# Four graph layers on one core: layer 2 mixes nodes before the product with W, takes its logits from dot products on VectorE, and every engine's blocks stand in another order

## The chip, the core and the metric
The kernel runs on one core of a Trainium2 chip. The metric is the device time of one execution in microseconds (us). Engine names in the profile: PE is TensorE (PEld its weight loads), DVE is VectorE, ACT is ScalarE, POOL is GpSimd, SP is SyncE.

## The reference
The input x is 128 graphs of 128 nodes with 256 features, adj is 128 dense 128 x 128 matrices. Four residual layers follow each other, each on `h = max(layernorm(x), 0)`. The change touches the second:

```python
Wh = jnp.einsum('bsi,io->bso', hidden_state, W)
Wh1 = Wh @ a[:OUT_F, :]
Wh2 = Wh @ a[OUT_F:, :]
e = Wh1 + jnp.swapaxes(Wh2, 1, 2)
e = jax.nn.leaky_relu(e, negative_slope=ALPHA)
attention = jnp.where(adjacent_matrix > 0.5, e, NEG_INF)
attention = jax.nn.softmax(attention, axis=1)
h_prime = jnp.einsum('bst,bto->bso', attention, Wh)
return jax.nn.elu(h_prime)
```

The first layer is a hypergraph convolution with a 512-wide hidden layer (W1, W2), the third a diffusion with three weight matrices, the fourth weights a value product by a softmax over the nodes. All of it is fp32.

## The kernel before
Graphs are taken in 32 groups of four. In round i the kernel works on five groups at once: `next` (group i+1: degrees of the hypergraph, normalised x, the product yT), `front` (group i: layer 1 and layer 2), `mid` (i-1: layer 3), `late` (i-2: first part of layer 4) and `tail` (i-3: its softmax, sum and store). Each engine has one `body(r)` in which the blocks of these groups stand in an order written out by hand, and it runs them strictly in that order; semaphores counted in graphs hold a block until its inputs exist and its buffer or PSUM bank (`BANK`) is free. `rounds` runs `first`, then rounds 0 to 3 unrolled, a loop, and the last four unrolled.

Products with weights go as three passes of fp32r (`split_product`: high with high, high with low, low with high), so every transposed activation is kept as a high part, which ScalarE copies out of PSUM, and a low part, which VectorE subtracts (`low_of_relu`, L1239). Products of two activations and transposes are plain fp32 (L328, L491, L400).

Layer 2 of `front` runs like this. VectorE adds the residual (L1478), takes the moments (L1329, L1333) and writes the centred h (L1347) in `front_ln1`. TensorE transposes h (`front_h1`, eight 128 x 128 transposes, L491), ScalarE and VectorE make h1T high and low (L885, L1239), TensorE multiplies by W with the two columns W a appended (`front_wh`, 24 matmuls of 258 columns), VectorE scales the two logit columns (`front_columns`, L1513), ScalarE scales wh (`keep_wh`, L851). TensorE spreads one logit column over the partitions (`front_b1`, L400), VectorE forms logits, leaky relu and maximum (L1496, L1502, L1508), ScalarE the exponential (L940), VectorE scales the weights (`front_scale`, L1524), and TensorE applies them to wh (`front_att`, four fp32 products of 256 columns). The elu (L1412, L945, L1419) and layer 3's norm follow, and TensorE transposes layer 3's h (`mid_h2`) behind the four blocks `front_w1`. GpSimd does the rsqrts (`rsqrt`: L1083, L1085) and the elementwise sums, two tensors from SBUF each (L1090 to L1141). In VectorE's and SyncE's order `adj_f` of the next group is loaded only when `front_penalty` (L1378) has read the old one.

## Time and profile before
| what | value |
|---|---|
| time, median of 3 runs (lowest, highest) | 1487.95 us (1487.61, 1488.96) |
| profiled execution, first to last instruction | 1487.0 us |
| busy TensorE, VectorE, ScalarE, GpSimd | 96%, 81%, 66%, 64% |
| chain that ended last: TensorE, ScalarE, VectorE | 75%, 11%, 5% |
| granted TensorE clock | 0.989 of full |

The profile's page and its views show one execution, whose span of 1487.0 us is 0.95 us under the median of the runs. Busy shares are averages; an instruction's length includes a fixed part that overlaps its neighbour, so what an instruction costs its engine is the distance from start to start in the timeline.

### The profile page before, as it was taken

Reading aid. Unit: us, or ns where it says so; the run is one execution under the profiler, and the core shown is the slowest. Engines: PE = TensorE matmul, PEld = TensorE weight load, DVE = VectorE, ACT = ScalarE, POOL = GpSimd, SP = SyncE. Lnnn points to the kernel's source line nnn. Section 1 sums busy time; section 2 is a strip of 40 time slices with the busy share of each in tenths; the row PEclk is TensorE's granted clock in tenths of the full one; section 3 lists DMA queues with packets and bytes.
Section 4 is the critical chain, followed back from the end, with each engine's and each line's share of the span. In section 5 each row is a group of like instructions: output and inputs, shape, how many; then the busy total and the mean of one; then the engine's idle time right before and its main releaser. Section 6 shows DMA issues by size and latency. Waiting matters only on the chain.

```text
span 1487.0 us, 33717 instructions
## 1 busy us (share of the span) xinstructions
PE 1423.5 (96%) x8920; PEld 1263.7 (85%) x8920; DVE 1206.8 (81%) x4621; ACT 978.8 (66%) x2122; POOL 949.7 (64%) x974
## 2 busy tenths in 40 slices
PE   6799999999999999999999999999999999999975
PEld 5679988889888988988888988888988888988864
DVE  5778888888888888888888888888888888888773
ACT  4456667766667776667776666776666776666754
POOL 4555775666776666676666676675677666677524
PEclk9899999999999999999999999999999999999997
DMA  4001111101111110111110111110111110111001
GB/s 128 22 15 37 37 42 44 49 32 46 35 48 36 49 47 30 35 49 35 49 49 28 42 42 35 49 49 28 45 39 35 49 49 28 49 35 41 23 29 50
DMA packets 75372, 62.01 MB, mean 42 GB/s; under 512 B 3014, under 2 KB 70986, under 8 KB 75339
## 3 DMA queue, kind: packets, MB, share of 16 engines
q1 hardware_dynamic: 75338, 61.63, 12.7%
q8 instruction: 14, 0.23, 0.1%
q14 instruction: 20, 0.16, 0.0%
HBM read 36.45 MB, written 16.78 MB: 36 GB/s over the span
## 4 chain that ended last, share of the span: by engine, by line
PE 75%; ACT 11%; issue 5%; DVE 5%; DMA 1%; POOL 0%; DVEq 0%; ACTq 0%; POOLq 0%; SPq 0%
PE ps L343 35%; PE ps L347 18%; PE ps L328 16%; PE ps L491 4%; ACT wh L851 3%; ACT pT L940 3%; ACT h L918 2%; ACT h2T_hi L881 1%; ACT p L929 1%; PE ps L400 1%; ACT yT_hi L953 1%; DMA x_in<-in_x 1%; DVE stats L1329 1%; DVE h L1347 1%; DVE binc_T L1368 0%
## 5 line engine op out<-in xcount | busy, mean ns | idle before, releaser
L1130 POOL TENSOR_TENSOR x3n<-p,x 128x512 f32<-128x512 f32 x64 | 80.8, 1285 | 252.8 <-ACT p L929 252.8
L851 ACT ACTIVATE p<-ps,rs 128x512 f32<-128x512 f32 (+1 forms) x256 | 138.2, 582 | 106.4 <-PE ps L347 73.7
L1090 POOL TENSOR_TENSOR hT_lo<-hT,hT_hi 128x512 fp32r<-128x512 f32 x126 | 162.8, 1294 | 68.5 <-ACT hT_hi L871 65.4
L1085 POOL TENSOR_TENSOR rs<-var_e,neg_half 128x4 f32<-128x4 f32 x160 | 164.9, 1031 | 23.7
L343 PE MATMUL ps<-wl_hi,h2T_hi 128*128 128x258 f32 (+1 forms) x512 | 148.5, 371 | 7.8 <-ACT h2T_hi L881 7.2
L328 PE MATMUL ps<-p,alT 128*128 128x256 f32 (+1 forms) x512 | 136.9, 390 | 3.3 <-DVE h3T_lo L1239 2.3
L343 PE MATMUL ps<-wl_lo,h2T_hi 128*128 128x258 f32 (+1 forms) x512 | 132.9, 341 | 0.0
L347 PE MATMUL ps<-wl_hi,h2T_lo 128*128 128x258 f32 (+1 forms) x512 | 132.4, 340 | 0.0
L949 ACT ACTIVATE h3T_hi<-ps 128x512 fp32r<-128x512 f32 x64 | 38.0, 594 | 139.0 <-PE ps L491 138.9
L491 PE MATMUL ps<-ident,h 128*128 128x128 f32 x768 | 118.3, 278 | 9.9 <-DVE h L1347 9.4
L491 PEld LDWEIGHTS ps<-ident,h 128*128 128x128 f32 x768 | 92.3, 142 | 32.9 <-issue 10.4
L1347 DVE TENSOR_SCALAR_CACHE_REDUCE h<-x,mv 128x256 f32<-128x256 f32 x256 | 113.6, 463 | 2.3
L1329 DVE BATCH_NORM_STATS2 stats<-x 128x6 f32<-128x256 f32 x256 | 109.2, 426 | 5.5
L1117 POOL TENSOR_TENSOR alT<-zb,adj_m 128x512 f32<-128x512 f32 x32 | 41.1, 1285 | 113.1 <-DVE zb L1438 113.1
L328 PEld LDWEIGHTS ps<-p,alT 128*128 128x128 f32 x512 | 86.4, 190 | 15.7 <-issue 4.8
L343 PEld LDWEIGHTS ps<-wl_hi,h2T_hi 128*128 128x128 f32 x512 | 81.0, 191 | 21.2 <-issue 17.0
L347 PEld LDWEIGHTS ps<-wl_hi,h2T_lo 128*128 128x128 f32 x512 | 88.5, 190 | 11.6
L343 PEld LDWEIGHTS ps<-wl_lo,h2T_hi 128*128 128x128 f32 x512 | 88.4, 190 | 11.3
L851 ACT ACTIVATE vqk<-ps,rs 128x384 f32<-128x384 f32 x128 | 73.9, 577 | 33.8 <-PE ps L347 33.7
L871 ACT ACTIVATE hT<-ps,cols_sb 128x512 f32<-128x512 f32 x128 | 88.1, 689 | 6.6 <-PE ps L347 1.5
L1105 POOL TENSOR_TENSOR x<-x 128x512 f32<-128x512 f32 x64 | 82.0, 1282 | 13.3 <-ACT x L851 13.3
L871 ACT ACTIVATE hT_hi<-ps,cols_sb 128x512 fp32r<-128x512 f32 x128 | 87.6, 684 | 0.1
(178 smaller groups left out, 4476.0 us busy)
## 6 DMA issues: line engine op xcount, KB each, us to landing
x_in<-in_x SPq DMA_DIRECT2D x32, 512.0 KB, 3.9
out_x<-x SPq DMA_DIRECT2D x32, 512.0 KB, 2.9
adj_f<-in_adjT SPq DMA_DIRECT2D x32, 256.0 KB, 2.9
adj_m<-in_adjT SPq DMA_DIRECT2D x32, 256.0 KB, 2.8
adj_l<-adj_m SPq DMA_DIRECT2D x32, 256.0 KB, 2.3
vqk<-in_l_wk SPq DMA_DIRECT2D x3, 256.0 KB, 5.2
x<-in_w2T SPq DMA_DIRECT2D x1, 512.0 KB, 5.1
x<-in_w1T SPq DMA_DIRECT2D x1, 512.0 KB, 5.9
```

Source lines behind the costliest of these rows:

```text
L328: last = pe.matmul(dst, lhsT(c), rhs(c), start=(c == 0), stop=(c == chunks - 1))
L343: pe.matmul(dst, lhsT(a, c), rhs(b, c), start=(a == b == c == 0), stop=False)
L347: last = pe.matmul(dst, lhsT(1 - late, c), rhs(late, c), start=False, stop=(c == chunks - 1))
L491: last = pe.transpose(bank(name, b)[:, ((g % 2) * KC + c) * P:((g % 2) * KC + c + 1) * P], h[:, g, c * P:(c + 1) * P], ident[:])
L851: return act.activation(dst, src, ACT.Copy, scale=scale)
L871: act.activation(dst[:, hc, :], bank("u", hc), ACT.Relu, bias=cols_sb[:, 0, hc:hc + 1]).then_inc(S[ready], 1)
L1085: pool.tensor_tensor(rs[:, layer, :], var_e[:, layer, :], neg_half[:], ALU.pow).then_inc(done, G)
L1090: pool.tensor_tensor(hTs[1][:, hc, :], hT[:, hc, :], hTs[0][:, hc, :], ALU.subtract).then_inc(S["hT_lo"], 1)
L1105: pool.tensor_tensor(x4[:, s], x4[:, s], x3[:, s], ALU.add).then_inc(S["x4_ready"], 2)
L1130: pool.tensor_tensor(x3n[:, s], p0[:, s], x2[:, s], ALU.add).then_inc(S["x3_ready"], 2)
L1329: dve.bn_stats(stats[:, layer, g, :], src[:, g, :]).then_inc(st, 1)
L1347: dve.tensor_scalar(dst[:, g, :], src[:, g, :], mv[:, layer, g, 0:1], None, ALU.subtract, ALU.add, accum_out=unread[:, layer, g:g + 1]).th ...
```

## The change
Layer 2 is regrouped: softmax(e) (h W) is computed as (softmax(e) h) W. ScalarE now writes h1r = relu(x1 - mean) (`centre`), TensorE multiplies it by the attention weights straight into transposed form (`front_mix`, eight fp32 products of 128 columns), and `front_att` becomes the three-pass product with W (24 matmuls of 256 columns). `front_h1`, `front_wh` and `keep_wh` are gone. The two logits of a node are dot products of h1r with rows of W a that were spread over all partitions once (`va`, made by `third_rows`): `front_dots`, eight instructions on VectorE per round with both operands in SBUF. The rsqrt of the norm goes into the logits and into the softmax weights (one more small multiplication per pair). Moments of layers 1, 3 and 4 are taken in pairs of graphs. PSUM banks are dealt out anew, many waits are dropped, round 0 has a list of its own (`opening`), VectorE's body begins with `next_count` and ends with work of the next round (`ahead`), and GpSimd's begins with work of the round before (`past`).

```diff
-        BANK = {"u": (0, 4, 3, 2), "y": (0, 7), "s": (4, 5), "d": (0,), "c2": (6, 5), "h1": (7, 1), "wh": (2, 3, 4,
-                5), "b1": (6,), "att": (1, 5), "h2": (4, 3), "p2": (4, 5, 6, 7), "p10": (7, 6, 7, 6), "b2": (5,),
-                "z": (1, 2, 3, 4), "ap": (0, 1, 2, 3), "az": (0, 3), "h3": (0, 5), "vqk": (4, 1, 6, 7), "ak": (6,),
-                "row": (1,), "turn": (7,)}
+        BANK = {"u": (6, 7, 0, 3), "y": (7, 6), "s": (5, 6), "d": (7,), "c2": (1, 3), "b1": (5,), "att": (3, 1),
+                "h2": (1, 7), "p2": (4, 5, 6, 7), "p10": (2, 7, 4, 3), "b2": (0,), "z": (1, 2, 3, 4),
+                "ap": (0, 1, 2, 3), "az": (0, 4), "h3": (5, 6), "vqk": (5, 6, 4, 5), "ak": (5,),
+                "row": (0,), "turn": (2,), "yA": (1, 2)}
...
+            def load_x(r):
+                if not r.steady and r.i in (0, 1,):
+                    wait(sp, S["h0_ready"], r.front(G))
+                if not r.steady and r.i in (0, 1,):
+                    wait(sp, S["xb_ready"], r.front(G))
+                sp.dma_start(x_in[:], group(x, r.i + 1)).then_inc(S["x_loaded"], 16)
...
+            def third_rows(r):
+                pe.wait_ge(S["dotted"], 2 * KC)
+                for k in range(2):
+                    for c in range(KC):
+                        last = spread(ps[:, 5, (k * KC + c) * P:(k * KC + c + 1) * P], att_cols[:, c, k:k + 1])
+                last.then_inc(S["va_spread"], 1)
...
-            def front_h1(r, b):
-
...
-            def front_wh(r, g):
...
-                split_product(bank("wh", g)[:, 0:D + 2], lambda a, c: h1Ts[a][:, g, c, :],
-                              lambda b, c: wl1s[b][:, c, :], KC,
-                              0, (S["h1T_lo"], r.front(2 * (g // 2) + 2))).then_inc(S["wh_ready"], 1)
+            def front_mix(r, b):
+                for g in (2 * b, 2 * b + 1):
+                    pe.wait_ge(S["h1_ready"], r.front(g + 1))
+                    pe.wait_ge(S["pT_scaled"], r.front(g + 1))
+                    for c in range(KC):
+                        at = ((g % 2) * KC + c) * P
+                        last = product(bank("yA", b)[:, at:at + P], lambda k: h1r[:, g, c * P:(c + 1) * P],
+                                       lambda k: pT[:, g, :], 1)
+                    last.then_inc(S["h1T_ready"], 1)
 
             def front_b1(r):
-
+                wait(pe, S["vqk_copied"], r.late(1))
                 pe.wait_ge(S["wh12_ready"], r.front(G))
...
             def front_att(r, g):
-
-                pe.wait_ge(S["wh_kept"], r.front(g + 1))
-                pe.wait_ge(S["pT_scaled"], r.front(g + 1))
-                if g == 0:
-                    wait(pe, S["h1T_lo"], r.front(G))
-                elif g == 2:
-                    wait(pe, S["wh_kept"], r.front(G))
-                product(bank_pair("att", g), lambda c: pT[:, g, :],
-                        lambda c: wh[:, g, :], 1).then_inc(S["att_ready"], 1)
+                if not r.steady and r.i == 0:
+                    pe.wait_ge(S["weights_lo"], 1)
+                pe.wait_ge(S["h1T_copied"], r.front(2 * (g // 2) + 2))
+                split_product(bank_pair("att", g), lambda a, c: h1Ts[a][:, g, c, :], lambda b, c: wl1s[b][:, c, :], KC,
+                              0, (S["h1T_lo"], r.front(2 * (g // 2) + 2))).then_inc(S["att_ready"], 1)
...
-            def keep_wh(r, g):
-
-                wait(act, S["att_ready"], r.mid(g + 1))
-                act.wait_ge(S["wh12_ready"], r.front(G))
-                scaled(wh[:, g, :], bank("wh", g)[:, 0:D], rs[:, 1, g:g + 1]).then_inc(S["wh_kept"], 1)
+            def relu_p0(r, b):
+                s = slice(2 * b, 2 * b + 2)
+                act.wait_ge(S["vb_ready"], r.mid(2 * b + 2))
+                act.activation(p0[:, s], p0[:, s], ACT.Relu).then_inc(S["relu_ready"], 2)
...
+            def centre(layer, src, dst, b, value, ready, done):
+                act.wait_ge(ready, value(2 * b + 2))
+                for g in (2 * b, 2 * b + 1):
+                    act.activation(dst[:, g, :], src[:, g, :], ACT.Relu,
+                                   bias=nmean[:, layer, g:g + 1]).then_inc(done, 1)
+
+            def front_centre(r, b):
+                centre(1, x1, h1r, b, r.front, S["nm1_ready"], S["h1_ready"])
...
+            def moments(layer, src, gs, value, st, ag):
...
+                dve.wait_ge(st, value(gs[-1] + 1))
                 dve.memset(c0[:, 0:1], 0.0).then_inc(S["filled"], 1)
...
+            def spread_about(layer, src, b, value, st, ag, done):
+                gs = slice(2 * b, 2 * b + 2)
+                moments(layer, src, (2 * b, 2 * b + 1), value, st, ag)
+                dve.wait_ge(ag, value(2 * b + 2))
+                dve.tensor_scalar(nmean[:, layer, gs], mv[:, layer, gs, 0], -1.0, None, ALU.mult).then_inc(done, 2)
...
-            def front_penalty(r):
-
-                dve.wait_ge(S["adj_f_loaded"], r.loads(r.i))
+                moments(0, x_in, range(G), r.next, S["st0"], S["ag0"])
+
+            def next_penalty(r):
+                dve.wait_ge(S["adj_f_loaded"], r.loads(r.i + 1))
...
+            def front_residual(r, b):
+                s = slice(2 * b, 2 * b + 2)
+                dve.wait_ge(S["res0_ready"], r.front(2 * b + 2))
+                dve.wait_ge(S["c2_ready"], r.front(2 * b + 2))
+                dve.tensor_tensor(x1[:, s, :], bank("c2", b).rearrange("p (g d) -> p g d", g=2),
+                                  res0[:, s, :], ALU.add).then_inc(S["x1_ready"], 2)
+
+            def front_ln1(r, b):
+                dve.wait_ge(S["x1_ready"], r.front(2 * b + 2))
+                spread_about(1, x1, b, r.front, S["st1"], S["ag1"], S["nm1_ready"])
...
+            def front_dots(r, b):
+                flat = q[:].rearrange("p g c -> p (g c)")
+                for g in (2 * b, 2 * b + 1):
+                    dve.wait_ge(S["h1_ready"], r.front(g + 1))
+                    for k, done in enumerate((S["dot_a"], S["dots_ready"])):
+                        if g > 0:
+                            dve.wait_ge(done, r.front(g))
+                        dve.tensor_tensor_reduce(flat[:, k * D:(k + 1) * D], h1r[:, g, :], va[:, k * D:(k + 1) * D],
+                                                 1.0, 0.0, ALU.mult, ALU.add,
+                                                 wh12r[:, g, k:k + 1]).then_inc(done, 1)
+
             def front_columns(r):
                 dve.wait_ge(S["rs1_ready"], r.front(G))
-                dve.wait_ge(S["wh_ready"], r.front(G))
-                dve.tensor_tensor(wh12[:], four("wh")[:, :, D:D + 2], rs[:, 1, :].rearrange("p (g a) -> p g a", a=1)
+                dve.wait_ge(S["dot_a"], r.front(G))
+                dve.wait_ge(S["dots_ready"], r.front(G))
+                dve.tensor_tensor(wh12[:], wh12r[:], rs[:, 1, :].rearrange("p (g a) -> p g a", a=1)
                                   .broadcast_to((P, G, 2)), ALU.mult).then_inc(S["wh12_ready"], G)
 
             def front_inverse(r, b):
                 s = slice(2 * b, 2 * b + 2)
                 dve.wait_ge(S["pT_ready"], r.front(2 * b + 2))
-                dve.reciprocal(rz[:, s], zsum[:, s]).then_inc(S["rz_ready"], 2)
+                dve.reciprocal(rz[:, s], zsum[:, s]).then_inc(S["rz_a"], 2)
+                dve.wait_ge(S["rz_a"], r.front(2 * b + 2))
+                dve.tensor_tensor(rz[:, s], rz[:, s], rs[:, 1, s], ALU.mult).then_inc(S["rz_ready"], 2)
```

The new order of TensorE: w1 (0 to 2), h2 (0), w1 (3), h2 (1), p2 (0, 1), row, p10 (0), w2 (0), p2 (2, 3), w2 (1, 2), w2_low (0), b2, w2 (3), w2_low (1 to 3), sums, h3 (0, 1), p10 (1), s (0, 1), c2 (0 to 3), turn, p10 (2, 3), ap (0), vqk (0), d, ap (1 to 3), vqk (1), b1, y (0), vqk (2, 3), y (1), az (0 to 2), mix (0), az (3), mix (1), ak, att (0 to 3).

The new order of VectorE: next_count, tail_max, next_inverse, late_ln3 (1), mid_columns, next_binc, next_moments, tail_norm, mid_edges, front_variance, late_low (0, 1), front_z (0 to 3), next_degrees, front_residual (0, 1), front_ln1 (0, 1), tail_out, front_dots (0, 1), front_columns, next_gt, z1_scale, front_logits (0, 1), front_leaky (0), mid_z1 (0), front_max (0), front_leaky (1), mid_z1 (1), front_max (1), mid_z1 (2), front_weights (0), mid_z1 (3), front_weights (1), y_low (0), front_low (0), mid_vb (0, 1), front_low (1), y_low (1), elu_low (0), mid_vb (2, 3), elu_high (0), elu_low (1), mid_ln2 (0), elu_high (1), mid_ln2 (1), mid_low (0), next_penalty, tail_weights, tail_sum, late_ln3 (0), mid_low (1).

The new order of GpSimd: add_res0 (0), then of the round before add_xb (1), add_x4 (1), add_bias (1), add_x3 (0), then add_res0 (1), add_x3 (1), mid_scale, front_lo (0 to 3), add_squares (0, 1), join_squares, next_scale, front_scale0, mask_edges, shift_x, late_scale, add_bias (0), front_scale1, add_xb (0), add_x4 (0).

## Rows read from the trace of the kernel before

**Rows 1.** The page, busy time of TensorE and VectorE over the span.
```profile
PE 1423.5 (96%) x8920; PEld 1263.7 (85%) x8920; DVE 1206.8 (81%) x4621; ACT 978.8 (66%) x2122; POOL 949.7 (64%) x974
```

**Rows 2.** The view by windows: rounds 3 to 30, then the rest (columns: window, length, busy time and count of each engine, clock, DMA).
```profile
146.32:1387.08 1240.76, 1226.60 (x7786) 1095.76 (x7785) 1040.04 (x4005) 849.99 (x1848) 824.60 (x841) 1.00 0.13 42
...
1387.08:1487.00 99.92, 74.97 (x414) 63.24 (x412) 58.54 (x206) 51.96 (x111) 44.26 (x43) 0.89 0.10 32
```

**Rows 3.** TensorE's timeline, one steady round: start, length, instruction (four lines, the h1 transposes around one product of h3).
```profile
709.66 0.60 PE L491 MATMUL ps<-ident,h 128*128 128x128 f32 x4
...
710.02 0.60 PE L343 MATMUL ps<-wl_hi,h3T_hi 128*128 128x384 f32 x2
...
710.46 0.51 PE L343 MATMUL ps<-wl_lo,h3T_hi 128*128 128x384 f32 x2
...
711.15 0.60 PE L491 MATMUL ps<-ident,h 128*128 128x128 f32 x4
```

**Rows 4.** TensorE's timeline, same and next round: y products, attention product, h2 and h3 transposes.
```profile
716.59 1.05 PE L328 MATMUL ps<-gt,h 128*128 128x128 f32 x8
...
717.48 1.03 PE L328 MATMUL ps<-p,alT 128*128 128x256 f32 x4
...
720.13 1.04 PE L328 MATMUL ps<-wh,pT 128*128 128x256 f32 x4
...
721.32 1.10 PE L328 MATMUL ps<-wh,pT 128*128 128x256 f32 x4 [0.15 <-ACT wh L851]
...
727.84 1.20 PE L491 MATMUL ps<-ident,h 128*128 128x128 f32 x8
...
729.28 0.70 PE L343 MATMUL ps<-wl_hi,h2T_hi 128*128 128x512 f32 x2 [0.24 <-ACT h2T_hi L881]
...
744.21 0.60 PE L491 MATMUL ps<-ident,h 128*128 128x128 f32 x4
...
745.04 1.11 PE L328 MATMUL ps<-p,alT 128*128 128x257 f32 x4 [0.23 <-DVE h3T_lo L1239]
```

**Rows 5.** VectorE's timeline, same round: last aggregate of layer 1, first elu, the longest of five waits.
```profile
708.64 0.17 DVE L1333 BATCH_NORM_AGGREGATE mv<-stats 128x2 f32<-128x6 f32 x1
...
721.48 0.68 DVE L1412 SCALAR_TENSOR_TENSOR el<-ps,x 128x512 f32<-128x512 f32 x1
...
733.69 0.29 DVE L1356 TENSOR_SCALAR_CACHE_REDUCE inc_T<-adj_f 128x128 f32<-128x128 f32 x1 [1.68 <-DMA adj_f<-in_adjT]
```

**Rows 6.** VectorE's timeline, opening: two of the dot products with one operand in PSUM, and a wait.
```profile
24.79 0.41 DVE L1276 CUSTOM_DVE_ANT_0 zb<-p,ps 128x256 f32<-128x256 f32 x1
...
25.24 0.42 DVE L1276 CUSTOM_DVE_ANT_0 zb<-p,ps 128x256 f32<-128x256 f32 x1
...
32.59 0.29 DVE L1356 TENSOR_SCALAR_CACHE_REDUCE inc_T<-adj_f 128x128 f32<-128x128 f32 x1 [5.07 <-DMA adj_f<-in_adjT]
```

**Rows 7.** VectorE by line and form, all rounds: leaky relu of q, and centring.
```profile
L1502 DVE SCALAR_TENSOR_TENSOR pT<-q 128x256 f32<-128x256 f32 x64 | 26.6, 416 | 0.1
...
L1347 DVE TENSOR_SCALAR_CACHE_REDUCE h<-x,mv 128x256 f32<-128x256 f32 x256 | 113.6, 463 | 2.3
```

**Rows 8.** VectorE's timeline, opening: instructions with both operands, or one at double rate, in SBUF.
```profile
22.16 1.01 DVE L1235 TENSOR_TENSOR hT_lo<-hT,hT_hi 128x512 fp32r<-128x512 f32 x1 [1.94 <-ACT hT_hi L871]
...
23.63 1.24 DVE L1235 TENSOR_TENSOR hT_lo<-hT,hT_hi 128x512 fp32r<-128x512 f32 x1 [0.46 <-ACT hT L871]
...
26.69 0.83 DVE L1378 TENSOR_SCALAR pen<-adj_f 128x512 f32<-128x512 f32 x1
```

**Rows 9.** GpSimd's timeline, opening: beside them.
```profile
22.57 1.75 POOL L1136 TENSOR_TENSOR res<-xb,h 128x512 f32<-128x512 f32 x1
```

**Rows 10.** GpSimd's timeline, one steady round: from layer 1's rsqrt on.
```profile
709.38 1.04 POOL L1085 TENSOR_TENSOR rs<-var_e,neg_half 128x4 f32<-128x4 f32 x1
...
710.39 1.30 POOL L1141 TENSOR_TENSOR p<-p,bk 128x512 f32<-128x512 f32 x1
...
711.63 1.30 POOL L1122 TENSOR_TENSOR xb<-x_in,b2m 128x512 f32<-128x512 f32 x1
```

More of the change, by code:

```diff
@@ new lines, in store, with hand_adj, load_mask @@
+            def store(r):
+                sp.wait_ge(S["x4_ready"], r.tail(G))
+                sp.dma_start(group(out, r.i - 3), x4[:]).then_inc(S["stored"], 16)
+            def hand_adj(r):
+                wait(sp, S["al_ready"], r.mid(G))
+                wait(sp, S["ak_ready"], r.late(G))
+                sp.dma_start(adj_l[:], adj_m[:]).then_inc(S["adj_l_loaded"], 16)
+            def load_mask(r):
+                if r.steady or r.i > 0:
+                    sp.wait_ge(S["adj_l_loaded"], r.loads(r.i - 1))
+                sp.dma_start(adj_m[:], group(adjT, r.i)).then_inc(S["adj_m_loaded"], 16)
@@ L841, in first @@
                 next_y(r, 1)
-                first_rows(r)
             pe.wait_ge(S["consts_made"], 4)
-            rounds(pe, body, first)
+            rounds(pe, body, opening, first)
         @block.scalar
@@ L1073, in first @@
                 l1_hi()
-            rounds(act, body, first)
+            rounds(act, body, opening, first)
         @block.gpsimd
@@ L1175, in body @@
             def body(r):
+                past = r.later(-1)
+                if r.has_front:
+                    add_res0(r, 0)
+                if past.has_next:
+                    add_xb(past, 1)
+                if past.has_tail:
+                    add_x4(past, 1)
+                if past.has_mid:
+                    add_bias(past, 1)
+                    add_x3(past, 0)
+                if r.has_front:
+                    add_res0(r, 1)
+                if past.has_mid:
+                    add_x3(past, 1)
+                if r.has_mid:
+                    mid_scale(r)
                 if r.has_front:
@@ L1227, in _ @@
             constants()
-            rounds(pool, body, first)
+            rounds(pool, body, opening, first)
         @block.vector
```

895 lines of the change are left out of this document (428 added, 467 removed).

## Prediction, made before the changed kernel ran

> **What bounds the kernel now.** I read the page's busy shares first, then the windows by round, then TensorE's and VectorE's timelines of one steady round, and last GpSimd's. TensorE is busy 96% of the span [rows 1]. Rounds 3 to 30 take 1240.76 us, 44.31 each, at the full clock (1.00); per round TensorE is busy 43.8 us, VectorE 37.1, ScalarE 30.4, GpSimd 29.5 [rows 2]. A busy TensorE is not one at its peak, so I take its blocks from start to start. Four transposes and six matmuls of 384 columns fill 1.49 us; four of the matmuls take 0.69, six 1.04, so four transposes cost 0.45 [rows 3]. Priced so, one round holds 42.3 us of TensorE work and 2.0 of stalls. Three stalls stand out: eight transposes of h2 last until the next product starts 1.44 us later instead of 0.90 (0.5 lost, ScalarE's copy of h2T); two attention products take 1.19 where 0.86 is the price of the like-sized product before them (0.3, keep_wh); the last h3 transposes take 0.83 instead of 0.45 (0.4, VectorE's h3T_lo) [rows 4]. TensorE sets the round; VectorE has 7.2 us free.
>
> **The change, part by part.**
>
> TensorE. `front_h1` goes: -0.90 us. `front_att` as four fp32 products (1.72) becomes `front_mix`, eight of 128 columns, priced by the y products of the same form, 0.89 for four [rows 4]: +0.06. The 24 passes with W lose two columns each, nothing. The three stalls go: behind h2 (1) now stand p2 (0, 1), which need only the pair copied before w1 (3); keep_wh is gone; between h3 and ap stand p10 (1) and s. Together TensorE would need 41.5 us of work and some 0.4 of small losses, 41.9.
>
> VectorE. From the first elu (721.48) to the last aggregate of layer 1 in the next round (708.64 + 44.51) lie 31.7 us [rows 5], of which 3.5 are five waits, the longest 1.68 for adj_f. The rest, 28.2, changes so: y_low, z1_scale, two mid_z1 and tail_out move out of the stretch (-2.0), three centrings of about 0.4 go to ScalarE (0.463 long, less the overlap [rows 7]; -1.2), two mid_vb and the degrees come in (+1.5), the split into pairs adds a pause and a memset for each half (+0.6), and z waits about 0.25 for its rsqrt (var, then two low parts of 0.6 cover the rest). That is 27.4 us, with no outside wait in it: `next_penalty` is early, so adj_f lands before `next_count`.
>
> The dots. A dot product of 256 took 0.42 us and the next began 0.45 after it, with a wait on itself and one operand in PSUM [rows 6]. The new ones wait on the dot before last, so 0.36 to 0.45 each; eight take 3.2 us, with nmean and tail_out before them. ScalarE's centring runs beside; it has 14 us free per round.
>
> The shared path between VectorE and GpSimd is what I price separately. In the opening hT_lo, both operands in SBUF, took 1.01 and 1.24 us at a size that costs 0.6 to 0.7, and pen took 0.83 against its usual 0.42 [rows 8]; GpSimd's sum at 22.57 took 1.75 instead of 1.30 [rows 9, 10]. The ends agree: hT_lo ends 0.6 after GpSimd's next sum is first seen, and the second hT_lo ends 0.55 after that sum's end at 24.32. So one of the two stands still until the other's instruction is done. The Trainium skill says the same ("SBUF — State Buffer", SBUF: two separate sides: an exclusive lock between a VectorE instruction with two SBUF inputs and a GpSimd instruction, held for the whole instruction); by that rule, the trace agrees. In before nothing steady collides, since the leaky relu of q stands where GpSimd idles.
>
> In after it collides. After the last aggregate (E = 0) GpSimd needs about 1.6 us for its rsqrt and then has six sums of 1.3 us ready back to back (add_xb, add_x4, add_res0, add_xb, add_x4, add_bias) [rows 10], until about 11 us. VectorE runs dots 0.35 to 3.5, then `front_columns` (both operands now in SBUF), then logits, two leaky relus and two rz products. What a collision costs is between nothing and one sum (1.3) per VectorE instruction. I take that VectorE, whose next dot starts before the last one has ended, keeps the path through the dots (nearest row: the pen and hT_lo pairs, one wait each), and that each later single instruction waits for the running sum: front_columns ends at 4.65 instead of 3.4, the first leaky relu loses 0.4, the second 0.6, the rz product about 0.2.
>
> The round then: TensorE's `front_b1` starts 4.75 after E; from it to the second attention pair's first half are b1 0.46, y 1.78, twelve matmuls of 384 at 2.08, az 1.72, mix 1.78, ak 0.84, att 1.46, in all 10.1. On that path mix (0) waits 1.1 for its weights, which the leaky relus delayed, and a hand-over costs 0.2: the elu starts 16.2 after E. 27.4 + 16.2 = **43.6 us per round** against 44.31. VectorE is then busy about 41 us and sets the round.
>
> The rotation of the lists, the new banks and dropped waits I cost at nothing beyond this: in the walk through the round no bank wait came last by more than 0.2 us. They would cost up to the stalls that they replace (1.2). The softmax path got an extra ScalarE copy, a low part and a 2.9 us product behind mix, covered by az (3), mix (1) and ak. SyncE's store stands behind the copy of adj_l and the load of adj_m; the buffers have over 20 us until they are wanted.
>
> Sum on the profiled span: 28 rounds x 0.7 = 20; rounds 1 and 2, less full, 1; the opening saves the 5.07 us wait for adj_f [rows 6] but its dots meet GpSimd's wide_lows, so 2 of it (0 to 5); the end [rows 2] 1 (-2 to 3). 1487.0 - 24 = 1463.0, and about 1 us more in the median: **1464 us**.
>
> A second rule of the skill speaks against the dots: "Vector Engine (DVE) Microarchitecture Reference", Points that are easy to get wrong, has a scalar-tensor-tensor with two non-bf16 SBUF sources at half throughput. The leaky relu of q has such sources and takes 0.416 us for 256 elements, as with one in PSUM, so the trace disagrees. By the rule eight dots would cost 8 x 0.27 = 2.1 us more and the round 45.7; the sum goes without it.
>
> **The rivals.**
>
> A, no collision that matters: the dots' second operand does not share the path, or GpSimd's sums come when VectorE reads PSUM. Then E to elu is 3.4 + 0.1 + 10.1 + 0.3 = 13.9, VectorE's cycle 41.3, and TensorE's 41.9 to 42.5 sets the round: 30 x 2.1 + 3 = 66 at most, 50 at least, 1421 to 1437, say 1427. Against it speak rows 8 and 9.
>
> B, slower: GpSimd gets the path between any two dots. From the fifth dot on (E + 1.8) each waits for one sum: dots 4 to 7 and front_columns, five waits of 1.3 less the one already counted, 5.2, less the leaky relus' 1.0 that then no longer meet a sum. The round is 43.6 + 4.2 = 47.8, and 1487 + 30 x 3.5 - 3 = 1589. The point from which it decides: more than one sum slips in between dots. For it speaks that at 22.57 VectorE got the path between two back-to-back GpSimd sums, so the mirror case is likely; against it that dots overlap each other by 0.07.
>
> B', the same with some sums not ready in time (add_x4 waits for ScalarE's weigh): one to three extra waits, 44.9 to 46.5 per round, 1500 to 1545.
>
> C, stalls return in other places and take 0.7: the round stays at 44.3, 1484 to 1490.
>
> **How the numbers follow.** Forecast (1440 to 1483) 0.43; A 0.20; C 0.04; B' 0.15; B 0.18. The likeliest is 1464, its own range 1440 to 1483. The range reaches to A and B' and leaves out B and the tails: 1418 to 1550. A measurement of this kernel tells 0.2% (3 us) from no change: faster 0.63, same 0.04, slower 0.33.
>
> **What would show it.** The changed profile should have 512 instead of 768 transposes; dots of 0.42 us except those that meet a GpSimd sum, up to 1.7; a front_columns and leaky relus with lengths above 0.17 and 0.42; GpSimd sums above 1.3 us; a round near 43.6 with VectorE over 90% busy. If all dots are 0.42, A holds; if the last four are each over 1.5 us, B. The forecast is wrong from the start if VectorE shows outside waits of over 1 us before E, or if TensorE stalls elsewhere than at b1 and mix.

## The result and the profile after

The changed kernel takes 1629.12 us (median of 4 runs, 1626.97 to 1630.14) against 1488.06 beside it: a ratio of 1.0943, 95% interval 1.0929 to 1.0957. It is slower by 141 us where 24 less were forecast. The profiled execution has a span of 1628.4 us; TensorE's busy share fell from 96% to 89% and VectorE's rose from 81% to 87% [rows 1].

The view by windows of the changed kernel: 28 rounds, from one `next_d` to another (columns as in [rows 2]).

```profile
142.40:1510.87 1368.47, 1242.00 (x7786) 1130.46 (x7784) 1229.24 (x4511) 851.30 (x1874) 841.56 (x839) 0.95 0.11 37
```

1368.47 / 28 = 48.87 us per round, against 44.31 [rows 2]: 4.56 more, 128 of the 141 us. The rest, 14 us, is ahead of these rounds and behind them: 259.9 us against 246.2. The mean clock of the rounds is 0.95 instead of 1.00.

VectorE's timeline of one steady round (start, length, engine, line, operation, tiles). E, the last aggregate of layer 1, starts at 727.23.

```profile
727.69 0.42 DVE L1459 CUSTOM_DVE_ANT_0 q<-h1r,va 128x256 f32<-128x256 f32 x1
...
728.73 0.42 DVE L1459 CUSTOM_DVE_ANT_0 q<-h1r,va 128x256 f32<-128x256 f32 x1
...
729.08 1.49 DVE L1459 CUSTOM_DVE_ANT_0 q<-h1r,va 128x256 f32<-128x256 f32 x1
...
733.33 1.47 DVE L1459 CUSTOM_DVE_ANT_0 q<-h1r,va 128x256 f32<-128x256 f32 x1
...
734.95 1.00 DVE L1467 TENSOR_TENSOR wh<-wh12r,rs 128x8 f32<-128x8 f32 x1
```

Dots 1 to 4 take 0.42 us and start 0.35 apart. Dots 5 to 8 take 1.47 to 1.50, and `front_columns` takes 1.00 for eight columns, where it took 0.17 in the kernel before. GpSimd's timeline of the same stretch:

```profile
727.96 1.04 POOL L1006 TENSOR_TENSOR rs<-var_e,neg_half 128x4 f32<-128x4 f32 x1
728.98 1.30 POOL L1058 TENSOR_TENSOR xb<-x_in,b2m 128x512 f32<-128x512 f32 x1
730.25 1.47 POOL L1041 TENSOR_TENSOR x<-x 128x512 f32<-128x512 f32 x1
...
734.49 1.44 POOL L1041 TENSOR_TENSOR x<-x 128x512 f32<-128x512 f32 x1
735.88 1.26 POOL L1075 TENSOR_TENSOR p<-p,bk 128x512 f32<-128x512 f32 x1
```

Read the two together. The first sum starts at 728.98, dot 5 at 729.08; the sum ends at 730.28, the dot at 730.57, the second sum at 731.72, dot 6 at 732.00, and so on: one of each in turn, four dots and `front_columns` against five sums. A dot grows by 1.07 us, a sum by some 0.15 (1.44 to 1.47 instead of 1.30), and the last sum, with no partner, takes 1.26.

TensorE's timeline of that stretch (in brackets the idle time and what ended it), and the windows behind it:

```profile
731.05 0.51 PE L359 MATMUL ps<-wl_hi,h3T_lo 128*128 128x384 f32 x2
736.09 1.09 PE L414 MATMUL ps<-ident,wh 128*128 128x128 f32 x4 [4.53 <-DVE wh L1467]
736.97 1.91 PE L340 MATMUL ps<-gt,h 128*128 128x128 f32 x8
```

```profile
735.50:737.00 1.50, 0.91 (x5) 0.94 (x6) 1.29 (x4) 0.00 (x0) 1.50 (x2) 0.58 0.00 0
737.00:738.50 1.50, 1.50 (x9) 1.50 (x9) 1.28 (x5) 0.00 (x0) 0.15 (x1) 0.50 0.00 0
738.50:740.00 1.50, 1.50 (x9) 1.50 (x9) 1.50 (x5) 1.02 (x2) 0.00 (x0) 0.78 0.00 0
```

`front_b1` waits 4.53 us for the columns; in the kernel before b1 had no such wait. Then comes a second loss: behind the idle stretch the granted clock is 0.50 (1.2 instead of 2.4 GHz) for about 3 us (the window from 738.50 is half at either level), b1 takes 1.09 instead of 0.65 and the eight y products 1.91, with 1.57 from their start to the next product against 0.89 at the full clock. In the next two rounds TensorE worked for about 6 and 3.4 us at the low level, so round lengths repeat as 48.4, 49.7, 48.7.

What the change was to bring on TensorE is there:

```profile
704.92 0.65 PE L461 MATMUL ps<-ident,h 128*128 128x128 f32 x4
705.32 0.71 PE L355 MATMUL ps<-yT_hi,w_hi 128*128 128x512 f32 x2
...
718.86 1.07 PE L461 MATMUL ps<-ident,h 128*128 128x128 f32 x8
719.68 0.71 PE L355 MATMUL ps<-wl_hi,h2T_hi 128*128 128x512 f32 x2
```

Four transposes of h2 give way to the next product after 0.40 us, eight of h3 after 0.82; the stalls of [rows 4] behind them are gone.

### The profile page after: what moved, and what is told of

It is laid out like the page before. It is cut to its first block, busy times and chain, and to the rows that moved or that the text cites. A ratio compares the mean times of both kernels' runs of the same rounds, so it can differ in the third digit from the quotient of the medians.

```text
span 1628.4 us, 33172 instructions
## 1 busy us (share of the span) xinstructions
PE 1443.7 (89%) x8924; PEld 1305.7 (80%) x8924; DVE 1416.3 (87%) x5196; ACT 982.3 (60%) x2154; POOL 969.9 (60%) x974
## 4 chain that ended last, share of the span: by engine, by line
PE 70%; DVE 19%; issue 9%; ACT 1%; POOL 0%; DVEq 0%; DMA 0%; POOLq 0%; ACTq 0%; SPq 0%
PE ps L355 30%; PE ps L340 19%; PE ps L359 14%; DVE q L1459 7%; DVE stats L1274 4%; PE ps L461 3%; PE ps L414 3%; DVE wh L1467 2%; DVE x L1420 1%; DVE wh12r L1459 1%; DVE mv L1279 1%; DVE z L1413 0%; DVE mv L1276 0%; DVE nmean L1293 0%; DVE wcol L1504 0%
## 5 line engine op out<-in xcount | busy, mean ns | idle before, releaser
L1459 DVE CUSTOM_DVE_ANT_0 q<-h1r,va 128x256 f32<-128x256 f32 x256 | 219.7, 921 | 0.0
L847 ACT ACTIVATE yT_hi<-ps 128x512 fp32r<-128x512 f32 x64 | 37.9, 593 | 202.6 <-PE ps L340 202.6
L1004 POOL TENSOR_SCALAR var_e<-mv 128x4 f32<-128x4 f32 x128 | 31.4, 245 | 203.5 <-DVE mv L1279 201.1
L414 PE MATMUL ps<-ident,wh 128*128 128x128 f32 x128 | 30.4, 382 | 136.4 <-DVE wh L1467 136.4
L414 PEld LDWEIGHTS ps<-ident,wh 128*128 128x128 f32 x128 | 19.9, 192 | 145.9 <-issue 140.3
L1041 POOL TENSOR_TENSOR x<-x 128x512 f32<-128x512 f32 x64 | 91.7, 1435 | 11.4 <-ACT x L751 11.4
L340 PE MATMUL ps<-gt,h 128*128 128x128 f32 x512 | 96.3, 352 | 0.9 <-DVE gt L1351 0.9
L857 ACT ACTIVATE h1r<-x,nmean 128x256 f32<-128x256 f32 x128 | 57.8, 499 | 64.9 <-DVE nmean L1293 64.9
L355 PE MATMUL ps<-wl_hi,h3T_hi 128*128 128x384 f32 x256 | 94.1, 455 | 0.3 <-DVE q L1438 0.2
L340 PEld LDWEIGHTS ps<-gt,h 128*128 128x128 f32 x512 | 91.1, 263 | 2.5 <-DVE gt L1351 1.4
```

Source lines behind the costliest of these rows:

```text
L340: last = pe.matmul(dst, lhsT(c), rhs(c), start=(c == 0), stop=(c == chunks - 1))
L355: pe.matmul(dst, lhsT(a, c), rhs(b, c), start=(a == b == c == 0), stop=False)
L414: return pe.transpose(dst, col.broadcast_to((P, P)), ident[:])
L857: act.activation(dst[:, g, :], src[:, g, :], ACT.Relu, bias=nmean[:, layer, g:g + 1]).then_inc(done, 1)
L1041: pool.tensor_tensor(x4[:, s], x4[:, s], x3[:, s], ALU.add).then_inc(S["x4_ready"], 2)
L1459: dve.tensor_tensor_reduce(flat[:, k * D:(k + 1) * D], h1r[:, g, :], va[:, k * D:(k + 1) * D], 1.0, 0.0, ALU.mult, ALU.add, wh12r[:, g, k: ...
```

## The experiments

The theory, T: a VectorE instruction with both operands in SBUF and a sum on GpSimd exclude each other, and they take turns, one whole instruction of each, also between two VectorE instructions that follow each other at once. "Round" below is the mean of the last 25 of the 28 rounds, from the starts of `next_d` in each trace; 48.9 in the changed kernel, 44.3 before.

### The sums wait for the columns

```diff
                 if r.has_front:
                     front_scale1(r)
+                    pool.wait_ge(S["wh12_ready"], r.front(G))
                 if r.has_next:
                     add_xb(r, 0)
```

> One wait more than the changed kernel: GpSimd, after the rsqrt of layer 1, waits for the scaled columns (front_columns) before its six sums. Theory T (a GpSimd sum and a VectorE instruction with both operands in SBUF exclude each other, one whole instruction of each in turn): no sum is ready during the dots, so all eight dots are 0.42 us and start 0.35 apart, front_columns 0.17 instead of 1.00, TensorE's stall before b1 goes from 4.5 us to under 0.5 and the clock in b1 and y from 0.50 to 1.00. The leaky relus (E + 6 to E + 8) now fall beside the sums and may wait up to 1.3 us each, 0 to 1 of it on the path. Round 42.3 to 43.4 instead of 48.4, span 1450 to 1478. Rival R (the later dots are slow by themselves, or by ScalarE's centring beside them): dots 5 to 8 stay at 1.4 to 1.5 us, round 48.4 or more, span 1628 or more. Rival L (the new order of the lists costs, not the dots): dots get short but stalls appear elsewhere, round over 44.3, span over 1490.

Measured: 1472.08 us, ratio to the kernel before 0.9872 (0.9856 to 0.9888); span 1470.5, round 43.58. One wait on GpSimd takes 157 us from the changed kernel. All eight dots are 0.42, `front_columns` 0.17, TensorE waits for nothing before b1, and the rounds are at the full clock. The lists cost nothing that shows, so rival L is out, and so is R. The round is 0.2 above the range, since three instructions now meet sums (VectorE's timeline):

```profile
665.50 0.80 DVE L1445 SCALAR_TENSOR_TENSOR pT<-q 128x256 f32<-128x256 f32 x1
...
666.95 0.80 DVE L1445 SCALAR_TENSOR_TENSOR pT<-q 128x256 f32<-128x256 f32 x1
...
669.03 1.09 DVE L1476 TENSOR_TENSOR rz<-rz,rs 128x2 f32<-128x2 f32 x1
```

The leaky relus take 0.80 instead of 0.42 and the rz product, two columns wide, 1.09 instead of 0.16.

### Two sums beside the dots

```diff
                 past = r.later(-1)
+                if past.has_front:
+                    pool.wait_ge(S["wh12_ready"], past.front(G))
                 if r.has_front:
                     add_res0(r, 0)
```

> A dose: as the changed kernel, but GpSimd waits for the scaled columns after the first two of its six sums. Theory T (one of each in turn): exactly two of the eight dots are long (dots 5 and 6, 1.4 to 1.5 us), dots 7 and 8 are 0.42, front_columns 0.17. VectorE gives back 2 x 1.07 + 0.8 = 2.9 us per round, TensorE's stall before b1 goes from 4.5 to about 1.6, and up to 1.5 more comes back if the clock no longer falls; less up to 1 for leaky relus that now meet sums. Round 44.0 to 46.0, span 1500 to 1560. Rival R (slow for another reason than the sums): four long dots as before, span 1628 or more. Rival P (the sum only slows what runs beside it in proportion, no turns): all dots beside the two sums are stretched alike, no dot over 1 us.

Measured: 1509.35 us, ratio 1.0125 (1.0108 to 1.0141), round 44.82. VectorE's timeline:

```profile
723.51 1.48 DVE L1461 CUSTOM_DVE_ANT_0 q<-h1r,va 128x256 f32<-128x256 f32 x1
...
724.92 1.50 DVE L1461 CUSTOM_DVE_ANT_0 q<-h1r,va 128x256 f32<-128x256 f32 x1
...
726.36 0.41 DVE L1461 CUSTOM_DVE_ANT_0 q<-h1r,va 128x256 f32<-128x256 f32 x1
...
727.26 0.17 DVE L1469 TENSOR_TENSOR wh<-wh12r,rs 128x8 f32<-128x8 f32 x1
```

Two sums, two long dots (the leaky relus, which now meet sums too, take 1.07 and 0.79). The number of long dots is the number of sums that are ready; P and R would have shown eight stretched or four long ones.

### The sums cut in halves

```diff
-                pool.tensor_tensor(x4[:, s], x4[:, s], x3[:, s], ALU.add).then_inc(S["x4_ready"], 2)
+                for g in (2 * b, 2 * b + 1):
+                    pool.tensor_tensor(x4[:, g], x4[:, g], x3[:, g], ALU.add).then_inc(S["x4_ready"], 1)
```

(xb and res0 likewise.)

> The changed kernel with each x4, xb and res0 sum of 128x512 cut into two of 128x256, same order, same bytes. Theory T (one whole instruction of each in turn): a dot that meets a sum waits for a half one, about 0.65, so dots 5 to 8 start about 0.8 us apart instead of 1.42, and front_columns waits half as long: 2.9 us less per round, and up to 1.5 more if the clock stays up behind a stall of 1.6 instead of 4.5; half sums that are left may meet the leaky relus, 0.65 each at most. Round 44.5 to 46.2, span 1513 to 1565. Rival P (the two share by bytes, a dot is as slow as the total traffic beside it): dots stay at 1.4 us, round 48.4, span 1628.

Measured: 1501.85 us, ratio 1.0084 (1.0067 to 1.0100), round 44.62. VectorE's timeline:

```profile
719.54 0.94 DVE L1461 CUSTOM_DVE_ANT_0 q<-h1r,va 128x256 f32<-128x256 f32 x1
...
723.25 0.46 DVE L1469 TENSOR_TENSOR wh<-wh12r,rs 128x8 f32<-128x8 f32 x1
```

With the same bytes to add, a dot's delay fell from 1.07 to 0.52 us and that of `front_columns` from 0.83 to 0.29. So a dot waits for one instruction of GpSimd, and for half as long when that is half as long. The second leaky relu, which now meets a half sum too, takes 0.94 instead of 0.42. The span, 1499.8 us, is below the 1513 expected. Two of the 28 rounds took 45.94 instead of 44.5: in both the granted clock fell behind the stall of 1.83 us before b1 (window from one of them, columns as in [rows 2]).

```profile
1036.90:1040.30 3.40, 3.40 (x13) 3.40 (x12) 3.33 (x9) 2.34 (x8) 3.36 (x4) 0.50 0.00 0
```

### The dots' second operand in PSUM

```diff
+            def front_va(r):
+                wait(pe, S["p10_copied"], r.mid(3))
+                pe.wait_ge(S["z_ready"], r.front(G))
+                for k in range(2):
+                    for c in range(KC):
+                        last = spread(ps[:, 4, (k * KC + c) * P:(k * KC + c + 1) * P], att_cols[:, c, k:k + 1])
+                last.then_inc(S["va_back"], G)
...
-                        dve.tensor_tensor_reduce(flat[:, k * D:(k + 1) * D], h1r[:, g, :], va[:, k * D:(k + 1) * D],
+                        dve.tensor_tensor_reduce(flat[:, k * D:(k + 1) * D], h1r[:, g, :], second[:, k * D:(k + 1) * D],
```

> The changed kernel with its own order on GpSimd, but the dots read the spread rows of W a from PSUM: TensorE writes them there anew in each round (four transposes, 0.45 us, ahead of the first attention sum product). One operand of each dot in SBUF, one in PSUM. Theory T (only an instruction with both operands in SBUF takes turns with a sum): all eight dots 0.42 us with GpSimd's sums beside them at 1.27 to 1.30; front_columns still waits for one sum (up to 1.3), the leaky relus may wait too. TensorE's stall before b1 from 4.5 to about 0.5, clock 1.00. Round 43.0 to 45.0, span 1465 to 1530. Rival D (any dot takes turns, whatever its operands, since it is its output and accumulator or its first operand that counts): four dots of 1.4 to 1.5 us, round 48.4 to 49.3, span 1628 to 1660.

Measured: 1491.43 us, ratio 1.0015 (1.0006 to 1.0025), round 44.26. VectorE's timeline, then GpSimd's:

```profile
718.51 0.42 DVE L1475 CUSTOM_DVE_ANT_0 q<-h1r,ps 128x256 f32<-128x256 f32 x1
...
719.07 1.16 DVE L1483 TENSOR_TENSOR wh<-wh12r,rs 128x8 f32<-128x8 f32 x1
```

```profile
717.68 1.28 POOL L1052 TENSOR_TENSOR x<-x 128x512 f32<-128x512 f32 x1
718.91 1.28 POOL L1081 TENSOR_TENSOR res<-xb,h 128x512 f32<-128x512 f32 x1
```

The order on GpSimd is that of the changed kernel, the sums run beside the dots, and neither grows. Of the instructions in this stretch only `front_columns`, both of whose operands are still in SBUF, grows: it takes 1.16. So it is the second SBUF operand that counts, and D is out. The dots start 0.87 us late, behind the new transposes, which wait for ScalarE's copy of p10.

### Products in place of dots

```diff
-                        dve.tensor_tensor_reduce(flat[:, k * D:(k + 1) * D], h1r[:, g, :], va[:, k * D:(k + 1) * D],
-                                                 1.0, 0.0, ALU.mult, ALU.add,
-                                                 wh12r[:, g, k:k + 1]).then_inc(done, 1)
+                        dve.tensor_tensor(flat[:, k * D:(k + 1) * D], h1r[:, g, :], va[:, k * D:(k + 1) * D],
+                                          ALU.mult).then_inc(done, 1)
```

> The changed kernel with its own order on GpSimd, but the eight dots are plain products of the same operands (h1r and the spread rows, both in SBUF, 128x256, same waits between them) with no running sum and so no read of an accumulator behind each; the logits' columns are then left out (a constant stands in their place, the output differs). Theory T (any VectorE instruction with both operands in SBUF takes turns with a sum, also between two that follow each other at once): as with the dots, the products from the fifth on start about 1.4 us apart. Rival Q (a dot loses its turn because of the accumulator read that stands between two dots; products that follow each other directly keep the path, which is what I had forecast for the dots): all eight about 0.35 apart, front_columns waits for one sum, round near 43.6 to 44.5, span 1465 to 1500.

(The kernel leaves the logit columns out; a constant stands in their place.)

Measured: 1629.04 us (one run; span 1627.3), round 48.95. VectorE's timeline, the eight products in one row:

```profile
726.85 7.07 DVE L1460 TENSOR_TENSOR q<-h1r,va 128x256 f32<-128x256 f32 x8
734.05 1.01 DVE L1469 TENSOR_TENSOR wh<-wh12r,rs 128x8 f32<-128x8 f32 x1
```

They take 7.07 us, as the eight dots do (727.69 to 734.80). The accumulator read between dots has nothing to do with it: Q, which was my forecast in its purest form, is out.

### One operand on GpSimd's side

```diff
-                pool.tensor_tensor(res0[:, s], xb[:, s], h0[:, s], ALU.add).then_inc(S["res0_ready"], 2)
+                pool.tensor_scalar(res0[:, s], h0[:, s], 1.0, None, ALU.add).then_inc(S["res0_ready"], 2)
```

(x4 and xb likewise.)

> The other side of the pair: in the changed kernel GpSimd's x4, xb and res0 sums become additions of the constant 1.0 to one operand of the same size; the second summand of each is left out (its output differs). Theory T1 (only a GpSimd instruction with two operands in SBUF takes turns with VectorE): dots all 0.42 us, round 42.5 to 44.5. Theory T2 (every GpSimd instruction of this size does): from the fifth dot on each dot is its 0.35 plus one GpSimd addition, whatever that then takes; the bits of GpSimd's small operations on 128x4 did not show it, since they were done before a dot began or hold the path for a small part of their time.

The second summand of each is left out. Measured: 1444.6 us (one run; span 1442.8), round 42.60. VectorE's timeline, then GpSimd's:

```profile
693.51 0.42 DVE L1458 CUSTOM_DVE_ANT_0 q<-h1r,va 128x256 f32<-128x256 f32 x1
...
693.85 0.82 DVE L1458 CUSTOM_DVE_ANT_0 q<-h1r,va 128x256 f32<-128x256 f32 x1
...
694.61 0.41 DVE L1458 CUSTOM_DVE_ANT_0 q<-h1r,va 128x256 f32<-128x256 f32 x1
...
695.51 0.39 DVE L1466 TENSOR_TENSOR wh<-wh12r,rs 128x8 f32<-128x8 f32 x1
```

```profile
693.52 1.78 POOL L1058 TENSOR_SCALAR xb<-x_in 128x512 f32<-128x512 f32 x1
695.27 1.49 POOL L1041 TENSOR_SCALAR x<-x 128x512 f32<-128x512 f32 x1
```

These additions are even longer than the sums (1.49 us), and yet only one dot of eight grows, by 0.40, and `front_columns` by 0.22. (Later the second rz product grows by 0.27, but beside the bias sum, which still has two operands: it runs from 701.10 to 702.37, the product from 701.96 to 702.39.) T1 holds for nearly all of the cost, not for all of it: an addition of one operand stopped VectorE for a short part of its time. Which part is not settled. The Trainium skill ("SBUF — State Buffer", SBUF: two separate sides) has the lock between a VectorE instruction with two SBUF inputs and any GpSimd instruction that reads SBUF, for its whole length. For the sums that nearly fits: a dot and a sum in turn take 1.42 us from start to start, where they take 0.35 and 1.23 undisturbed (GpSimd's timeline above, 717.68 to 718.91). For these additions the measurement says otherwise.

### The stall filled

```diff
                 wait(pe, S["vqk_copied"], r.late(1))
+                if r.steady:
+                    for k in range(36):
+                        pe.transpose(bank("b1")[:, 0:C], ident[:], ident[:])
                 pe.wait_ge(S["wh12_ready"], r.front(G))
```

> The changed kernel with 36 transposes of the identity (about 4.0 us at the full clock, overwritten by b1) on TensorE in the stall before b1; nothing else. It prices the clock by itself. Theory K (the 3 us at the granted clock 0.50 behind the 4.5 us stall cost 1.5 us per round): dots as in the changed kernel, b1 back to 0.6 us for its four and y to 0.9 to 1.05, clock 1.00 all through, round 46.9 to 47.5 instead of 48.4, span 1588 to 1603. Rival V (behind b1 the softmax on VectorE and ScalarE sets the time, not TensorE): round 48.0 to 48.4, span 1617 to 1630. If the filling is longer than the stall, it costs what it is over.

Measured: 1584.93 us, ratio 1.0635 (1.0618 to 1.0653), round 47.13 (the 24 rounds with the filling alone), where the changed kernel has 48.9. TensorE's timeline:

```profile
717.34 4.09 PE L578 MATMUL ps<-ident 128*128 128x128 f32 x36
721.99 0.65 PE L414 MATMUL ps<-ident,wh 128*128 128x128 f32 x4 [0.56 <-DVE wh L1470]
722.58 1.16 PE L340 MATMUL ps<-gt,h 128*128 128x128 f32 x8
```

Work that nobody needs, put into an idle stretch, saves 1.8 us per round: the dots are as slow as before, but b1 takes 0.65 instead of 1.09 and y 0.92 instead of 1.57 to the next product, and the rounds with the filling are at 1.00. The expectation had 1.5, from a round with 3 us at the low clock; every third round has 6. So the span, 1583.1, came out 5 below its range.

### The sums behind the leaky relus

```diff
                     front_scale1(r)
+                    pool.wait_ge(S["lr_ready"], r.front(G))
+                if r.has_tail:
+                    add_x4(r, 0)
+                    add_x4(r, 1)
                 if r.has_next:
                     add_xb(r, 0)
-                if r.has_tail:
-                    add_x4(r, 0)
```

(x4 (1) is gone from its old place; xb (1) of the round before goes between the two x3 sums, and res0 (1) behind them.)

> GpSimd waits for both row maxima behind the leaky relus (not only for the columns), and then does the two x4 sums first; the second xb sum goes between the two x3 sums. Theory T: neither dots nor front_columns nor leaky relus meet a sum; only the two small products of rz (2 columns) can, up to 1.3 us each. Dots 0.42, leaky relus 0.41, E to the first elu 13.9 to 15.2, round 41.9 to 42.9 where TensorE sets it, span 1420 to 1455. Rival S (what the sums lose in time comes back elsewhere: they are late for keep_x3, the second vb pair or the x3 sums, and VectorE waits for GpSimd): a wait of 1 us or more on VectorE at elu_high or vb, round over 43.4, slower than the kernel whose sums wait only for the columns.

Measured: 1475.33 us, ratio 0.9899 (0.9883 to 0.9916), round 43.74: outside the range, and no better than the wait for the columns. It isn't rival S, no wait for GpSimd shows on VectorE. The leaky relus are back at 0.42 and the loss has moved on (VectorE's timeline):

```profile
668.58 0.96 DVE L1475 TENSOR_TENSOR rz<-rz,rs 128x2 f32<-128x2 f32 x1
...
670.77 1.23 DVE L1475 TENSOR_TENSOR rz<-rz,rs 128x2 f32<-128x2 f32 x1
```

Two products of two columns each, 0.16 us of work, wait 0.80 and 1.07. I had named them with up to 1.3 us each and then left them out of the range.

### The sums in the gaps

```diff
                     front_scale1(r)
+                    pool.wait_ge(S["wh12_ready"], r.front(G))
+                if r.has_tail:
+                    add_x4(r, 0)
+                if r.has_front:
+                    pool.wait_ge(S["lz"], r.front(G))
+                if r.has_tail:
+                    add_x4(r, 1)
+                if r.has_front:
+                    pool.wait_ge(S["rz_ready"], r.front(2))
                 if r.has_next:
                     add_xb(r, 0)
...
                 past = r.later(-1)
+                if past.has_front:
+                    pool.wait_ge(S["rz_ready"], past.front(G))
                 if r.has_front:
                     add_res0(r, 0)
```

(x4 (1) and xb (1) are gone from their old places; xb (1) stands between the two x3 sums, and res0 (1) behind them.)

> The sums placed between the instructions that they would meet: x4 (0) after the scaled columns, x4 (1) after the second leaky relu, xb (0) after the first rz product, res0 (0) and bias (1) after the second, xb (1) between the two x3 sums. Theory T: with the wait for the columns alone the leaky relus took 0.80 instead of 0.42 twice and the first rz product 1.09 instead of 0.16; here all of them keep their own length. Round 43.60 less 0.76 less 0.93 = 41.9 if VectorE's path sets it, 41.9 to 42.5 with TensorE's own floor; span 1419 to 1437. Rival S (sums that come late make others wait: keep_x3, the second vb pair, the x3 sums): VectorE or ScalarE shows waits for GpSimd of 1 us and more, round 43 to 44, span 1455 to 1480.

Measured: 1430.89 us, ratio 0.9612 (0.9596 to 0.9628), round 42.22. It beats both kernels: 58 us less than the one before, measured beside it, and 198 less than the changed one. VectorE's timeline, then the windows (28 rounds):

```profile
733.59 0.42 DVE L1451 SCALAR_TENSOR_TENSOR pT<-q 128x256 f32<-128x256 f32 x1
...
734.64 0.42 DVE L1451 SCALAR_TENSOR_TENSOR pT<-q 128x256 f32<-128x256 f32 x1
...
736.34 0.22 DVE L1482 TENSOR_TENSOR rz<-rz,rs 128x2 f32<-128x2 f32 x1
...
737.80 0.29 DVE L1482 TENSOR_TENSOR rz<-rz,rs 128x2 f32<-128x2 f32 x1
```

```profile
137.97:1320.26 1182.29, 1182.29 (x7785) 1078.70 (x7784) 1091.69 (x4511) 850.37 (x1874) 826.43 (x839) 1.00 0.13 43
```

TensorE is busy in all of the 1182.29 us, so it sets the round again. That took four waits on GpSimd and another order of its sums, and no faster instruction.

### One part alone: dots in the kernel before

```diff
+            def extra_dots(r):
+                flat = q[:].rearrange("p g c -> p (g c)")
+                for g in range(G):
+                    for k, done in enumerate((S["dz_a"], S["dz_b"])):
+                        if g > 0:
+                            dve.wait_ge(done, r.front(g))
+                        dve.tensor_tensor_reduce(flat[:, k * D:(k + 1) * D], x1[:, g, :], bw[:],
+                                                 1.0, 0.0, ALU.mult, ALU.add, dz[:, g, k:k + 1]).then_inc(done, 1)
...
                     front_ln1(r)
+                    extra_dots(r)
```

> One part alone: the kernel before, with eight dots added on VectorE behind layer 1's normalisation (x1 and b2 W, both in SBUF; results thrown away, nothing else changed, no sum moved). There GpSimd has two sums in that place, add_bias (1) at 710.39 and add_xb (1) at 711.63, against last centring at 709.26. Theory T: exactly two of the eight dots are long, 1.4 to 1.5 us; the dots cost VectorE 2.8 + 2.1 = 4.9 us, h1T_lo comes 3.6 to 3.9 later, round 45.0 to 47.0 instead of 44.3, span 1508 to 1568. Rival L (the long dots belong to the changed kernel's lists or its h1r): all eight at 0.42, round 44.3 to 45.3.

Measured: 1636.07 us, ratio 1.0993 (1.0950 to 1.1035), round 48.9. VectorE's timeline, then TensorE's:

```profile
734.85 1.50 DVE L1499 CUSTOM_DVE_ANT_0 q<-x,bw 128x256 f32<-128x256 f32 x1
...
736.28 1.48 DVE L1499 CUSTOM_DVE_ANT_0 q<-x,bw 128x256 f32<-128x256 f32 x1
...
737.70 0.41 DVE L1499 CUSTOM_DVE_ANT_0 q<-x,bw 128x256 f32<-128x256 f32 x1
```

```profile
738.91 0.80 PE L344 MATMUL ps<-wl_hi,h1T_hi 128*128 128x258 f32 x2 [3.04 <-DVE p L1451]
```

And with one line more, on GpSimd behind the rsqrt of layer 1:

```diff
+                    pool.wait_ge(S["dz_b"], r.front(G))
```

> As the last one, but GpSimd's two sums wait for the eighth dot. Theory T: eight dots of 0.42, 2.8 us in all, h1T_lo 1.4 to 1.7 later than in the kernel before, round 44.3 to 45.3, span 1487 to 1517, so 20 to 50 us less than with the sums beside the dots, for the same work. Rival W (the wait costs as much as the turns): same time as with the sums beside them.

Measured: 1540.79 us, ratio 1.0342 (1.0318 to 1.0367), round 45.8; all eight dots are 0.42. TensorE's timeline:

```profile
693.55 0.51 PE L344 MATMUL ps<-wl_hi,h1T_hi 128*128 128x258 f32 x2 [0.90 <-DVE p L1452]
```

The count is as T has it, two sums and two long dots, in a kernel with none of the change's lists, and the turns, with the clock that falls behind them, are worth 95 us. But both rounds came out above their ranges. The turns cost VectorE 2.15 us and the round 3.1: `front_wh` waits 3.04 us instead of 0.90, by the profile for `mid_z1`, which stands behind the dots on VectorE (not for h1T_lo, as I had it), and behind the longer stall its first two products take 0.80 instead of 0.51, the clock again (mean 0.959 over the run against 0.986). It doesn't fall in every round. The four rounds from 793.66 to 985.17 are at 1.00 throughout and take 47.9 each, 2.1 more than with the sums later: that is the turns, and the rest of the 3.1 is the clock.

### Loss and round of the kernels with the change's lists

"Lost to turns" is what VectorE's two-operand instructions of one steady round take beyond their own length (dots and leaky relus 0.42, columns 0.17, rz 0.16), added up from its timeline.

| kernel | lost to turns, us | round, us |
|---|---|---|
| changed | 4 x 1.06 + 0.83 = 5.1 | 48.9 |
| changed, stall filled | 5.1 | 47.1 |
| two sums beside | 3.2 | 44.8 |
| half sums | 2.9 | 44.6 |
| sums behind the leaky relus | 1.9 | 43.7 |
| sums behind the columns | 1.7 | 43.6 |
| products in place of dots | 5.0 | 48.95 |
| dots' second operand in PSUM | 1.7 (and 0.9 waiting for its rows) | 44.3 |
| one operand on GpSimd | 0.9 | 42.6 |
| sums in the gaps | 0.2 | 42.2 |

The rounds at the full clock lie within 0.5 us of 42.0 plus the loss; so does the kernel with the dots' operand in PSUM, if its wait is added. Only the changed kernel and the one with products in place of dots, whose clock falls in the rounds, are off that line, by 1.8 and 1.9, and the filled stall gives the 1.8 back.

## Why the prediction was wrong

**What bounds it, and TensorE's part: right.** The transposes, the mix and the stalls came as worked out; the round without turns was put at 41.9 to 42.5 and is 42.2. The lists, banks and dropped waits, costed at nothing, cost nothing that any run shows.

**VectorE's stretch from elu to E: right.** 699.59 to 727.23 is 27.6 us, forecast 27.4. One slip stands in rival A's sum: its span goes by 2.1 us per round, the middle of its own 41.9 to 42.5; with 41.9 it reaches down to 1412.

**The dots' own price: right**, 0.42 each, 0.35 apart. The rule of the Trainium skill that was set against them ("Vector Engine (DVE) Microarchitecture Reference", Points that are easy to get wrong: half throughput for two SBUF sources that aren't bf16) would, by the estimate in the prediction, ask for 0.27 more, 0.69 each; undisturbed dots with both sources in SBUF take 0.42, as those with one in PSUM do.

**The failed step**, worth most of the miss, is "I take that VectorE, whose next dot starts before the last one has ended, keeps the path through the dots". It doesn't. A waiting sum got in between the dots, though they overlap by 0.07 us, and even between plain products: dots 5 to 8 took 1.47 to 1.50 us each instead of 0.42, and `front_b1` waited 4.53 us. The nearest row that I leaned on (hT_lo and pen, one wait each [rows 8]) couldn't tell, as no two such instructions stood there back to back with sums waiting. The row that could was GpSimd's: at 22.57 VectorE had slipped in between two of its sums [rows 9]. I named that mirror case as the argument for rival B and still gave B 0.18. Under the Trainium skill's page "SBUF — State Buffer" (SBUF: two separate sides) the lock is held for a whole instruction; read strictly, that leaves it free at every instruction's end, and there a waiting sum came in.

**Rival B came in**, with its place (dots 5 to 8 and the columns) and its sign: 47.8 per round and 1589 us were worked out. The filled stall has 47.1 and 1585. From E to the elu B had 47.8 less 27.4, 20.4 us, the trace 20.8 (727.23 to 747.99). That it comes so close is partly luck: its price per turn was too high (1.3 against 1.07 for a dot and 0.83 for the columns) and the clock was missing. At the full clock, in the kernel with the filled stall, the stretch is 19.5 (713.17 to 732.66).

**What nobody had in the sum** is the clock. B's stall before b1 was in the working, what follows a stall was not: 1.8 us per round, 50 in all. The kernel before had a granted clock of 1.00 in its rounds 3 to 30, but a row for it stood behind them, where the mean is 0.89 [rows 2]: on TensorE's timeline of the kernel before, after a stall of 4.41 us, eight transposes take 2.41 us that take 1.20 in a steady round [rows 4].

```profile
1434.60 2.41 PE L491 MATMUL ps<-ident,h 128*128 128x128 f32 x8 [4.41 <-DVE h L1347]
```

The prediction makes no use of it. The ends missed too: 2 us were to be saved in the opening, but there three of its dots meet the weights' low parts and take 1.39 each, and the rounds next to it had turns and the low clock already; 142.4 us ahead of the 28 rounds against 138.8, and 117.5 behind them against 107.5. How the 10 us behind them divide wasn't looked into.

The sum by the runs: 28 x (48.9 - 43.6) = 148 us of rounds and some 17 at the ends make the 165 between 1464 and 1629. Of the 5.3 per round 2.6 are turns beyond those in the forecast (5.1 against 2.5), 1.8 are clock, and 0.9 are spread over terms that no run separates. That the kernel whose sums wait for the columns takes 43.6, as forecast, is luck: it loses 1.7 to turns where the forecast had 2.5, and the rest of its round is 0.8 longer.

## What to carry to other kernels

Before putting an instruction with two SBUF operands on VectorE's critical path, list what GpSimd has ready at that moment: each such instruction, however small, can wait for most of one GpSimd sum of two operands (here up to 1.08 of 1.3 us), and a row of n of them for n sums. Put one operand in PSUM, or hold GpSimd back with a semaphore that fires behind the last of them, and place its sums one by one in stretches where no VectorE instruction has two operands in SBUF; if neither goes, cut the sums: halves halved the price here. And price a TensorE stall of 3 us or more with the low clock behind it: here 1.8 us per round behind 4.5, about 1 behind 3.0.
